# One stage for the combining of experts, the layer norm and most of h of an attention, in a two-layer graph and expert network

## The chip, the cores and the metric

The kernel runs on one core of one Trainium2 chip. The core has five engines with a program each: TensorE (PE; its weight loads have a row of their own, PEld), VectorE (DVE), ScalarE (ACT), GpSimd (POOL) and SyncE (SP), and sixteen DMA engines. Each engine runs its program in order; semaphores hold it where it needs another's result. The metric is the device time of one execution, in microseconds (us), lower is better.

## What is computed

1024 nodes with 512 features pass two layers; each is a graph step and an expert step on the layer norm of what came before. The change touches the end of the first expert step and the start of the second graph step:

```python
x = x + _L0_gnn_ref(_layernorm(x), ...)
x = x + _L0_ffn_ref(_layernorm(x)[None], ...)[0]     # 64 experts, two for each token
x = x + _L1_gnn_ref(_layernorm(x), ...)              # two attention layers of 8 heads
x = x + _L1_ffn_ref(_layernorm(x)[None], ...)[0]     # 8 experts, one for each token

# _L0_ffn_ref, after the experts:
out = jnp.einsum('bse,bsed->bsd', sparse_w, expert_out) + x
mu = out.mean(-1, keepdims=True)
var = ((out - mu) ** 2).mean(-1, keepdims=True)
return (out - mu) * jax.lax.rsqrt(var + EPS) * gamma + beta

# gat_conv in _L1_gnn_ref:
h = (x @ W).reshape(N, heads, out_ch)
a_src = jnp.einsum('nhc,hc->nh', h, att_src)
a_dst = jnp.einsum('nhc,hc->nh', h, att_dst)
e = jax.nn.leaky_relu(a_src[src] + a_dst[dst], NEG_SLOPE)
```

Everything is float32. The edges lie in a dense 1024 x 1024 matrix of counts, so the attention is dense too.

## The kernel before, in words

The nodes lie in eight tiles of 128 rows (`NT`), one row to a partition. The program is a row of stages (`nc.Block()`), each with a part for every engine, and a barrier between two stages. Order inside a stage is as written, engine by engine. The stages around the change:

- `layernorm("ln1")`, then `routing("rt0")`: TensorE makes the logits of the eight tiles, VectorE picks two experts for each token, TensorE counts ranks within the experts (L649, L651) from the picks (semaphore `s_pick`), VectorE turns them into row numbers, and GpSimd scatters the sixteen half sets of rows (L630). SP loads the weights of the first eight experts meanwhile (`first_experts`), and behind them a block of rows (L621).
- `experts("x0")` and a stage for overflowing experts (L1062 on).
- The combining stage (L1153 on). GpSimd gathers each tile's two expert rows into `yb`, four tiles ahead; TensorE makes the bias product of each tile (L1217); VectorE adds these to `xln` with their weights and takes the statistics; when all eight tiles are done, one square root, one scale, and then the tiles are scaled by gamma and added to `x`, to which GpSimd has added beta (L1187). Beside that TensorE, ScalarE and SP make the attention vectors `v1` and `v2` of both attentions (W times att): sixteen chunks of 512 columns (`chunks`) are loaded (`wc`), transposed (L1196), copied (`wct`, L1245) and multiplied (L1211). Four chunks follow each bias product from the fourth on.
- `layernorm("ln2")`: again statistics over all tiles, one square root, and eight tiles to be normed, transposed and copied to `xT`.
- `attend("a1")`: the score rows (L1640) from `v` and `xT`, their copy `aTs`, and their transposes (`ab`); then h = x W in sixteen units of 512 columns (L1673), six of them ahead of the first pair (`H0`), ten behind given pairs (`H_AFTER`). A pair is a head with a source tile, 64 in all. For each, GpSimd (L1461), ScalarE (L1474), VectorE (L1574), ScalarE (L1481) and TensorE (L1688) work one after the other, several pairs at a time; VectorE also makes the row maxima of a later head (L1568), TensorE broadcasts a later head's score row when the maxima of the head before are done (L1656), and at each head's start VectorE waits for the last product of the head before (L1583).

A matrix product in float32 leaves two records in the trace; a transpose leaves one.

## Time and profile before

| | us |
|---|---|
| median of three runs | 1403.1 |
| lowest, highest | 1400.1, 1413.2 |
| the profiled run, its own time | 1406.6 |
| its span in the trace | 1404.9 |
| TensorE busy, weight loads busy | 1075.2, 740.1 |
| VectorE, ScalarE, GpSimd busy | 761.8, 514.6, 594.8 |
| routing of the first experts, to the next stage's start | 286.4 to 347.1 |
| combining stage | 615.6 to 694.7 |
| layer norm | 695.2 to 710.2 |
| first attention | 710.5 to 963.4 |

All durations are read from one profiled execution, and times of day in the text are microseconds from its span's start. Busy time says how long an engine had an instruction running, not that it set the end: that is read from the waits.

### The profile page before, as it was taken

Reading aid. Unit: us, or ns where it says so; the run is one execution under the profiler, and the core shown is the slowest. Engines: PE = TensorE matmul, PEld = TensorE weight load, DVE = VectorE, ACT = ScalarE, POOL = GpSimd, SP = SyncE. Lnnn points to the kernel's source line nnn. Section 1 sums busy time; section 2 is a strip of 40 time slices with the busy share of each in tenths; the row PEclk is TensorE's granted clock in tenths of the full one; section 3 lists DMA queues with packets and bytes.
Section 4 is the critical chain, followed back from the end, with each engine's and each line's share of the span. In section 5 each row is a group of like instructions: output and inputs, shape, how many; then the busy total and the mean of one; then the engine's idle time right before and its main releaser. Section 6 shows DMA issues by size and latency. Waiting matters only on the chain. (4 is left out here: it accounts for less than half of the span.)

```text
span 1404.9 us, 17550 instructions
## 1 busy us (share of the span) xinstructions
PE 1075.2 (77%) x5484; PEld 740.1 (53%) x5488; DVE 761.8 (54%) x1609; ACT 514.6 (37%) x710; POOL 594.8 (42%) x471
## 2 busy tenths in 40 slices
PE   3999379650999999968398888878887887533696
PEld 2444367550777777747246777763644342132463
DVE  6888465636333333333638777751777675653134
ACT  2333433220111111101236676772466667630010
POOL 1000645105555555443026876781576777402002
PEclk9999699855999999975589999999999999855796
DMA  3000000073699999643030111101011111003974
GB/s 101 0 1 0 1 0 0 1 255 122 202 298 300 303 304 302 200 148 113 0 92 16 46 46 31 46 16 65 28 45 31 45 43 40 0 9 108 336 253 158
DMA packets 112476, 144.28 MB, mean 103 GB/s; under 512 B 30184, under 2 KB 72776, under 8 KB 112408
## 3 DMA queue, kind: packets, MB, share of 16 engines
q1 hardware_dynamic: 96168, 118.47, 26.1%
q0 software_dynamic: 14080, 21.03, 4.5%
q10 hardware_dynamic: 2160, 3.93, 0.7%
q8 instruction: 35, 0.57, 0.2%
q14 instruction: 33, 0.27, 0.1%
HBM read 138.71 MB, written 29.81 MB: 120 GB/s over the span
## 5 line engine op out<-in xcount | busy, mean ns | idle before, releaser
L1461 POOL TENSOR_TENSOR am<-CT,qb 128x1024 f32<-128x1024 f32 x128 | 299.3, 2363 | 61.7 <-ACT PT L1481 37.3
L1574 DVE TENSOR_TENSOR am<-PS,am 128x1024 f32<-128x1024 f32 x128 | 156.6, 1223 | 74.8 <-ACT PS L1474 67.1
L1474 ACT ACTIVATE PS<-adb,ab 128x1024 f32<-128x1024 f32 x128 | 142.9, 1117 | 90.5 <-DVE am L1574 90.4
L1042 DVE COPY yo<-PS 128x512 f32<-128x512 f32 x79 | 54.7, 692 | 208.9 <-PE PS L980 200.6
L1568 DVE CUSTOM_DVE_ANT_0 masked<-PS,mask 128x1024 f32<-128x1024 f32 x128 | 156.1, 1220 | 19.0 <-issue 17.3
L972 PE MATMUL PS<-xgT,w1r 128*128 128x128 f32 x1264 | 155.7, 277 | 0.0
L1007 ACT ACTIVATE hT<-PS,b1T 128x128 f32<-128x128 f32 x158 | 49.5, 364 | 288.4 <-PE PS L972 250.7
L1688 PE MATMUL PS<-h,PT 128*128 128x129 f32 x1024 | 128.3, 282 | 33.0 <-ACT PT L1481 26.4
L972 PEld LDWEIGHTS PS<-xgT,w1r 128*128 128x128 f32 x1264 | 149.2, 194 | 1.2 <-issue 1.2
L980 PE MATMUL PS<-w2r,hT 128*128 128x512 f32 x316 | 148.6, 593 | 0.1
L1481 ACT ACTIVATE PT<-am,as 128x1024 f32<-128x1024 f32 x128 | 145.2, 1134 | 0.3 <-DVE am L1574 0.3
L1688 PEld LDWEIGHTS PS<-h,PT 128*128 128x128 f32 x1024 | 122.7, 196 | 41.7 <-issue 40.5
L1701 PE MATMUL PS<-PT,h 128*65 128x512 f32 x256 | 124.9, 620 | 23.5 <-ACT PT L1481 14.3
L914 POOL DMA_INDIRECT ys_scratch<-yo,r_rowsi x64 | 65.6, 1025 | 109.0 <-DVE yo L1042 98.8
L351 DVE TENSOR_SCALAR oh_src<-iota,eT 128x1024 f16 x164 | 78.8, 480 | 17.7 <-PE PS L479 11.4
L1033 DVE COPY xgT<-PS 128x512 f32<-128x512 f32 x79 | 53.9, 683 | 54.6 <-PE PS L963 52.1
L1701 PEld LDWEIGHTS PS<-PT,h 128*65 128x65 f32 x256 | 32.9, 140 | 95.7 <-issue 79.4
L963 PEld LDWEIGHTS PS<-ident,xg 128*128 128x128 f32 x316 | 39.6, 145 | 67.6 <-issue 32.8
L980 PEld LDWEIGHTS PS<-w2r,hT 128*128 128x128 f32 x316 | 54.1, 191 | 39.2 <-issue 38.7
L479 PE MATMUL PS<-oh_src,oh_dst 128*128 x328 | 73.5, 379 | 0.9 <-DVE oh_dst L353 0.3
L909 POOL DMA_INDIRECT xg<-xs_scratch,r_rowsi x64 | 65.0, 1015 | 21.2 <-issue 20.3
L172 PE MATMUL PS<-ident,xln 128*128 128x128 f32 x96 | 20.5, 389 | 66.3 <-DVE xln L153 65.9
(308 smaller groups left out, 1601.2 us busy)
## 6 DMA issues: line engine op xcount, KB each, us to landing
w1r<-in_L_ffn_W SPq DMA_DIRECT2D x79, 512.0 KB, 6.2
w2r<-in_L_ffn_W SPq DMA_DIRECT2D x79, 512.0 KB, 7.6
adb<-a_scratch SPq DMA_DIRECT2D x16, 512.0 KB, 4.1
qb<-q_scratch SPq DMA_DIRECT2D x14, 512.0 KB, 3.7
wc<-in_L_gnn_W SPq DMA_DIRECT2D x16, 256.0 KB
xg<-xs_scratch SPq DMA_DIRECT2D x15, 256.0 KB
ys_scratch<-yo ACTq DMA_DIRECT2D x15, 256.0 KB
x_res<-in_x SPq DMA_DIRECT2D x1, 2048.0 KB, 10.5
```

The costliest lines, as they stand in the source:

```text
L351: dve.tensor_scalar(oh_src[:, bass.ds(slot, 1), c, :], iota[:], eT[:, 0, c, bass.ds(q, 1)], None, ALU.is_equal)
L479: mm = pe.matmul(PS[:, 2 * (t % 2) + h, :], oh_dst[:, bass.ds(slot, 1), c, :], oh_src[:, bass.ds(slot, 1), c, h * 512:(h + 1) * 512], star ...
L914: pool.indirect_dma_start(ys[0:rows, :], bass.IndirectOffsetOnAxis(picked[:, e:e + 1], 0), yo[:, e % 4, :], None, bounds_check=rows - 1, o ...
L972: mm = pe.matmul(PS[:, 2 + j % 2, c * P:(c + 1) * P], w1r[:, j, k, c * P:(c + 1) * P], xgT[:, j % 2, k, :], start=(k == 0), stop=(k == KD ...
L980: mm = pe.matmul(PS[:, 4 + j % 2, :], hT[:, j % 2, c, :], w2r[:, j, c, :], start=(c == 0), stop=(c == HC - 1))
L1461: pool.tensor_tensor(am[:, k % RING, :], CT[:, s, :], qb[:, hd % 2, :], ALU.add).then_inc(s_sum, 1)
L1474: act.activation(RELU, adb[:, hd % 2, :], ACT.Relu, bias=ab[:, s, hd:hd + 1]).then_inc(s_relu, 1)
L1481: act.activation(PT[:, k % PR, :], am[:, k % RING, :], ACT.Exp, bias=as02[:, s, hd:hd + 1], scale=1 - NEG_SLOPE).then_inc(s_exp, 1)
L1568: dve.tensor_tensor_reduce(masked[:], ASB, mask[:, t, :], 1.0, -3.0e38, ALU.subtract, ALU.max, mrow[:, hd % 2, t:t + 1]).then_inc(s_max, 1)
L1574: dve.tensor_tensor(am[:, k % RING, :], RELU, am[:, k % RING, :], ALU.add).then_inc(s_all, 1)
L1688: mm = pe.matmul(PS[:, d // PER, (d % PER) * (CH + 1):(d % PER + 1) * (CH + 1)], PT[:, (NT * hd + s) % PR, d * P:(d + 1) * P], h[:, s, hd, :],
L1701: mm = pe.matmul(PS[0:CH + 1, half, :], h[:, s, hd, :], PT[:, (NT * hd + s) % PR, half * 512:(half + 1) * 512], start=(s == 0), stop=(s == ...
```

## The change

The attention vectors are made in the routing, by a new class `Vectors` with the old statements. TensorE runs five of the sixteen chunks between the logits and the ranks (`V_AHEAD`), and eleven behind the ranks. All sixteen chunks have their own buffer, loaded in four pieces ahead of the experts' weights; it lies where the experts' first matrices come, so those are loaded piece by piece, each when two more chunks are transposed.

The combining stage does, tile by tile, what three stages did: sum, layer norm with gamma and beta, the next layer norm, transposes to `xT`, the scores `ab` (now tokens on partitions), the first half of h, and a quarter of h (two of the other four heads). The eighth tile's h and the last two heads stay in the attention: two units ahead of the first pair, four behind pairs (0,1), (0,4), (1,4), (2,4). `layernorm("ln2")` is gone. In the attention eight transposes of `ab` take the place of the score products. Each square root is made for one tile.

```diff
@@ routing @@
+                    if vectors is not None:
+                        vectors.turn_att(pe)
+                        vectors.products(pe, 0, V_AHEAD)
                     pe.wait_ge(s_pick, 1)
...
+                    if vectors is not None:
+                        vectors.products(pe, V_AHEAD, len(vectors.chunks))
                     pe.wait_ge(s_sw, 1)
...
+                    if vectors is not None:
+                        vectors.move(act)
                     act.wait_ge(s_tw, 1)
@@ Vectors @@
+            def products(self, pe, first, last):
+                if first == 0:
+                    self.turned(pe, 0)
+                    pe.wait_ge(self.s_attm, 1)
+                for i in range(first, last):
+                    if i + 1 < len(self.chunks):
+                        self.turned(pe, i + 1)
+                    self.summed(pe, i)
@@ first_experts @@
             for e in range(WR):
-                load_weights(sp, ins["L0_ffn_W1"], ins["L0_ffn_W2"], slice(e, e + 1), e, s_w0)
+                sp.dma_start(w2r[:, e, :, :], ins["L0_ffn_W2"][e:e + 1].rearrange("o (k p) h -> p (o k) h", p=P)
+                             ).then_inc(s_w0[e], 16)
+            for e in range(WR):
+                sp.wait_ge(vectors.s_wt, 2 * e + 2)
+                sp.dma_start(w1r[:, e, :, :], ins["L0_ffn_W1"][e:e + 1].rearrange("o (k p) h -> p (o k) h", p=P)
+                             ).then_inc(s_w0[e], 16)
@@ combining stage, gpsimd @@
+                for t in range(4):
+                    gather(t)
                 pool.wait_ge(s_gb, 32)
                 for t in range(NT):
                     pool.tensor_tensor(x[:, t, :], x[:, t, :], beta[:], ALU.add).then_inc(s_beta, 1)
+                    if t + 4 < NT:
+                        gather(t + 4)
@@ combining stage, tensor @@
+                def bias(t):
+                    if t >= 2:
+                        pe.wait_ge(s_o, t - 1)
+                    pe.matmul(PS[:, t % 2, :], r0["swT"][:, t * P:(t + 1) * P], r0["b2s"][:], start=True,
+                              stop=True).then_inc(s_bias, 1)
+
+                bias(0)
+                bias(1)
                 for t in range(NT):
+                    if t + 2 < NT:
+                        bias(t + 2)
+                    pe.wait_ge(s_xln, t + 1)
...
+                    for k in range(KD):
+                        mm = pe.transpose(PS[:, 2 + t % 2, k * P:(k + 1) * P], xln[:, t, k * P:(k + 1) * P], ident[:])
+                    mm.then_inc(s_xt, 1)
+                    pe.wait_ge(s_xtm, t + 1)
...
+                        mm = pe.matmul(PS[:, 7, t * 2 * HEADS:(t + 1) * 2 * HEADS], xT[:, k, own], v1[:, k, :],
+                                       start=(k == 0), stop=(k == KD - 1))
+                    mm.then_inc(s_ab, 1)
+                    if t == NT - 1:
+                        continue
...
+                        mm = pe.matmul(PS[:, 4 + t % 2, :], xT[:, k, own], W1t[0][:, k, :],
+                                       start=(k == 0), stop=(k == KD - 1))
+                    mm.then_inc(s_h, 1)
...
+                        mm = pe.matmul(PS[:, 6, q], xT[:, k, own], W1t[1][:, k, :],
+                                       start=(k == 0), stop=(k == KD - 1))
+                    mm.then_inc(s_hq, 1)
@@ combining stage, scalar @@
+                root(0)
+                root(1)
                 for t in range(NT):
+                    act.wait_ge(s_stat2, t + 1)
+                    act.activation(sq2[:, t:t + 1], ve2[:, t:t + 1], ACT.Sqrt).then_inc(s_sqrt2, 1)
+                    if t + 2 < NT:
+                        root(t + 2)
+                    act.wait_ge(s_rs2, t + 1)
+                    act.activation(xln[:, t, :], x[:, t, :], ACT.Identity, bias=nmr2[:, t:t + 1],
+                                   scale=rs2[:, t:t + 1]).then_inc(s_xln, 1)
+                    if t:
+                        h_moved(t - 1)
+                    act.wait_ge(s_xt, t + 1)
+                    act.copy(by_tile(xT, t), PS[:, 2 + t % 2, :].rearrange("p (k n) -> p k n", k=KD)).then_inc(s_xtm, 1)
@@ combining stage, vector @@
+                def summed(t):
+                    o = o0[:, t % 4, :]
+                    dve.wait_ge(s_bias, t + 1)
+                    dve.tensor_tensor(o, PS[:, t % 2, :], xln[:, t, :], ALU.add).then_inc(s_o, 1)
+                    dve.wait_ge(s_o, t + 1)
+                    dve.wait_ge(s_yb[t % 4], 32 * (t // 4 + 1))
...
+                summed(0)
                 for t in range(NT):
+                    if t + 1 < NT:
+                        summed(t + 1)
+                    if t:
+                        scaled(t - 1)
+                    added(t)
+                scaled(NT - 1)
@@ attend @@
+                H0 = 2
+                H_AT = (0, 1), (0, 4), (1, 4), (2, 4)
```

In the vector part, `summed(t)` has three full-width operations and three for statistics; `added(t)` makes the first norm with gamma and adds it to `x` (two full-width operations, four small ones, statistics); `scaled(t)` is five small operations that make the second norm's scale and shift.

Where instructions move, as the two programs list them. TensorE in the routing, before, from the logits (`r_wg`) to the first ranks (`r_Mb`):

```order
L641 MATMUL PS<-r_wg,xT 128x64 x32
L651 MATMUL PS<-r_Mb,before 128x64
L649 MATMUL PS<-r_Mb,onesb 128x64
L651 MATMUL PS<-r_Mb,before 128x64
L649 MATMUL PS<-r_Mb,onesb 128x64 x2
```

The same place after the change, with the chunks' transposes (`wc`) and products (`wct`) in between:

```order
L647 MATMUL PS<-r_wg,xT 128x64 x32
L894 MATMUL PS<-ident,att_3512 128x16
L895 MATMUL PS<-ident,att_3513 128x8
L903 MATMUL PS<-ident,wc 128x128 x8
L918 MATMUL PS<-att1T,wct 128x2 x4
L903 MATMUL PS<-ident,wc 128x128 x4
L918 MATMUL PS<-att1T,wct 128x2 x4
L903 MATMUL PS<-ident,wc 128x128 x4
L918 MATMUL PS<-att1T,wct 128x2 x4
L903 MATMUL PS<-ident,wc 128x128 x4
L918 MATMUL PS<-att1T,wct 128x2 x4
L903 MATMUL PS<-ident,wc 128x128 x4
```

A fifth product follows, and then the ranks: six transposed and five multiplied chunks now stand ahead of them.

TensorE at the start of the combining stage, before: four bias products (`r_b2s`), then the chunks:

```order
L1217 MATMUL PS<-r_b2s,r_swT 128x512 x4
L1221 MATMUL PS<-ident,att_5850 128x16
L1222 MATMUL PS<-ident,att_5851 128x8
L1196 MATMUL PS<-ident,wc 128x128 x8
L1211 MATMUL PS<-att1T,wct 128x2 x4
```

And after the change, tiles 0 and 1 (`v_3508` is `v1`; `W1t_6106` and `W1t_6107` are the half and the quarter of W):

```order
L1309 MATMUL PS<-r_b2s,r_swT 128x512 x3
L1321 MATMUL PS<-ident,xln 128x128 x4
L1326 MATMUL PS<-v_3508,xT 128x16 x4
L1337 MATMUL PS<-W1t_6106,xT 128x512 x4
L1342 MATMUL PS<-W1t_6107,xT 128x256 x4
L1309 MATMUL PS<-r_b2s,r_swT 128x512
L1321 MATMUL PS<-ident,xln 128x128 x4
L1326 MATMUL PS<-v_3508,xT 128x16 x4
L1337 MATMUL PS<-W1t_6106,xT 128x512 x4
L1342 MATMUL PS<-W1t_6107,xT 128x256 x4
```

The bias product of tile 3 stands behind the quarter of tile 0; each later one, up to tile 7's, behind the quarter of the tile three before it.

## Rows read from the trace of the kernel before

**Rows 1.** Table by stage: us, busy of each engine, granted clock, DMA share, GB/s.

```profile
306.00:312.00 6.00, 0.00 (x0) 0.00 (x0) 5.45 (x31) 0.00 (x0) 0.00 (x0) 0.50 1.08 366
615.60:710.40 94.80, 62.16 (x242) 49.29 (x242) 48.12 (x93) 22.41 (x42) 25.45 (x25) 0.51 0.30 95
```

**Rows 2.** Timeline, start of the combining stage: start, duration, engine, line, operation.

```profile
615.63 7.16 PE L1217 MATMUL PS<-r_b2s,r_swT 64*128 64x512 f32 x8 [8.56 <-PEq L1064]
...
622.64 0.69 DVE L1269 TENSOR_TENSOR o<-PS,xln 128x512 f32<-128x512 f32 x1 [14.84 <-DMA yb<-ys_scratch,r_posi]
```

**Rows 3.** Timeline, TensorE's h records of 512 columns in the attention's prologue.

```profile
728.83 7.89 PE L1673 MATMUL PS<-W1t,xT 128*128 128x512 f32 x18
```

**Rows 4.** Timeline, VectorE over one tile of the combining.

```profile
667.84 0.69 DVE L1269 TENSOR_TENSOR o<-PS,xln 128x512 f32<-128x512 f32 x1 [8.70 <-PE PS L1217]
668.57 0.75 DVE L1270 SCALAR_TENSOR_TENSOR o<-yb,r_top,o 128x512 f32<-128x512 f32 x1
...
670.87 0.18 DVE L1276 BATCH_NORM_AGGREGATE mv<-st 128x2 f32<-128x6 f32 x1
```

**Rows 5.** Timeline, the small operations of the norm and ScalarE's pass.

```profile
682.70 0.20 DVE L1280 RECIPROCAL tq<-sq 128x8 f32<-128x8 f32 x1 [0.27 <-ACT sq L1250]
...
683.98 5.75 ACT L1253 ACTIVATE o<-o,shift,rs 128x512 f32<-128x512 f32 x8 [1.31 <-DVE shift L1286]
```

**Rows 6.** Timeline, transposes of the layer norm and the first copy.

```profile
702.86 5.29 PE L172 MATMUL PS<-ident,xln 128*128 128x128 f32 x24 [23.89 <-DVE xln L153]
704.01 0.59 ACT L162 COPY xT<-PS 128x512 f32<-128x512 f32 x1 [2.87 <-PE PS L172]
```

**Rows 7.** Timeline of the routing: logits, last exponential, first rank, first scatter, next stage.

```profile
290.67 13.91 PE L641 MATMUL PS<-r_wg,xT 128*128 128x64 f32 x64 [5.14 <-DMA r_b2s<-in_L_ffn_b]
...
305.32 0.35 ACT L666 ACTIVATE r_lg<-r_lg,r_nm 128x64 f32<-128x64 f32 x1 [1.27 <-DVE r_nm L689]
...
312.65 0.24 PE L651 MATMUL PS<-r_Mb,before 128*128 128x64 bf16 x1 [8.06 <-DVE r_Mb L710]
...
322.91 1.31 POOL L630 DMA_INDIRECT xs_scratch<-xln,r_posi  x1 [35.48 <-DVE r_posi L744]
...
347.07 1.81 POOL L902 MEMSET xg<- 128x2048 f32 x1 [3.56 <-POOLq L614]
```

**Rows 8.** Granted clock (the third column from the end) in half microseconds.

```profile
287.50:288.00 0.50, 0.00 (x0) 0.00 (x0) 0.00 (x0) 0.20 (x1) 0.00 (x0) 0.76 1.04 234
707.50:708.00 0.50, 0.50 (x5) 0.41 (x4) 0.00 (x0) 0.28 (x1) 0.00 (x0) 0.90 0.00 0
721.00:721.50 0.50, 0.50 (x2) 0.31 (x2) 0.36 (x2) 0.00 (x0) 0.50 (x1) 0.76 0.17 25
724.50:725.00 0.50, 0.50 (x3) 0.26 (x2) 0.46 (x4) 0.00 (x0) 0.00 (x0) 0.83 0.82 336
```

**Rows 9.** Timeline of the pairs: a late row broadcast, and VectorE's waits at head starts.

```profile
830.35 0.17 DVE L1583 TENSOR_SCALAR dn<-PS 128x9 f32<-128x9 f32 x1 [5.53 <-PE PS L1688]
...
848.34 1.03 PE L1656 MATMUL PS<-a,sel 80*128 80x512 bf16 x2 [2.86 <-DVE mrow L1568]
...
860.71 0.17 DVE L1583 TENSOR_SCALAR dn<-PS 128x9 f32<-128x9 f32 x1 [8.46 <-PE PS L1688]
...
934.78 0.17 DVE L1583 TENSOR_SCALAR dn<-PS 128x9 f32<-128x9 f32 x1 [1.95 <-PE PS L1688]
```

**Rows 10.** Timeline of the attention's start: score products, and the first pair's addition.

```profile
710.50 7.03 PE L1640 MATMUL PS<-xT,v 128*16 128x512 f32 x16 [0.93 <-PEq L126]
...
744.90 1.22 DVE L1574 TENSOR_TENSOR am<-PS,am 128x1024 f32<-128x1024 f32 x1
```

**Rows 11.** Timeline, ScalarE's copy of a chunk, one of sixteen.

```profile
661.89 0.59 ACT L1245 COPY wct<-PS 128x512 f32<-128x512 f32 x1 [1.87 <-PE PS L1196]
```

**Rows 12.** Timeline, GpSimd's additions of beta and a VectorE operation beside them.

```profile
637.59 9.84 POOL L1187 TENSOR_TENSOR x_res<-x_res,beta 128x512 f32<-128x512 f32 x8
...
644.75 3.23 DVE L1270 SCALAR_TENSOR_TENSOR o<-yb,r_top,o 128x512 f32<-128x512 f32 x1
```

More of the change, by code:

```diff
@@ L613, in routing @@
             LOGP = P.bit_length() - 1
+            V_AHEAD = 5
             with nc.Block() as block:
@@ L1155, in build @@
-        s_yb, s_gb = [sem(f"c0_yb{j}") for j in range(4)], sem("c0_gb")
-        s_bias, s_sum, s_stat, s_sqrt, s_chain = (sem("c0_" + k) for k in ("bias", "sum", "stat", "sqrt", "chain"))
-        s_scale, s_norm, s_beta, s_scaled = (sem("c0_" + k) for k in ("scale", "norm", "beta", "scaled"))
+        yb = place("yb", [P, 4, TOPK, D], F32, 145 * KIB)
+        o0 = place("o0", [P, 4, D], F32, 102 * KIB)
+        gamma = place("gamma", [P, D], F32, 199 * KIB + 512)
+        beta = place("beta", [P, D], F32, 201 * KIB + 512)
@@ new lines, in build @@
+        tq2 = place("tq2", [P, NT], F32, 97 * KIB + 384)
+        rs2 = place("rs2", [P, NT], F32, 97 * KIB + 416)
+        nmr2 = place("nmr2", [P, NT], F32, 97 * KIB + 448)
+        st2 = place("st2", [P, NT, 6], F32, 97 * KIB + 480)
+        assert 97 * KIB + 480 + 4 * NT * 6 <= 98 * KIB
+        phase()
+        s_yb, s_gb, s_w1t = [sem(f"c0_yb{j}") for j in range(4)], sem("c0_gb"), sem("c0_w")
+        s_bias, s_o, s_sum, s_beta, s_chain = (sem("c0_" + k) for k in ("bias", "o", "sum", "beta", "chain"))
@@ L1158, in build @@
+        s_stat, s_sqrt, s_stat2, s_sqrt2, s_rs2 = (sem("c0_" + k) for k in ("stat", "sqrt", "stat2", "sqrt2", "rs2"))
+        s_free, s_xln, s_xt, s_xtm = (sem("c0_" + k) for k in ("free", "xln", "turned", "moved"))
+        s_ab, s_h, s_hq, s_hm, s_hqm = (sem("c0_" + k) for k in ("ab", "h", "hq", "hm", "hqm"))
         with nc.Block() as block:
@@ L1230, in _ @@
             @block.scalar
             def _(act):
-                act.wait_ge(s_attp, 1)
-                act.wait_ge(s_zero, 1)
-                act.copy(att1T[:], PS[:, 4, 0:2 * HEADS])
-                for a in range(2):
-                    for half in range(2):
-                        own = slice(half * CH2, (half + 1) * CH2)
-                        last = act.copy(att2T[own, :, 2 * a + half], PS[own, 4, 2 * HEADS + a * HEADS // 2:
-                                                                         2 * HEADS + (a + 1) * HEADS // 2])
@@ L1240, in _ @@
-                last.then_inc(s_attm, 1)
-                for i in range(len(chunks)):
-                    act.wait_ge(s_wt, i + 1)
-                    if i >= 2:
-                        act.wait_ge(s_v, i - 1)
-                    act.copy(wct[:, i % 2, :], PS[:, 5 + i % 2, :]).then_inc(s_wtm, 1)
-                act.wait_ge(s_v, len(chunks))
-                act.copy(v1[:].rearrange("p k n -> p (k n)"), PS[:, 7, 0:KD * 2 * HEADS])
-                act.copy(v2[:].rearrange("p k n -> p (k n)"), PS[:, 7, KD * 2 * HEADS:(KD + KF) * 2 * HEADS])
@@ L1397, in _ @@
                 def _(sp):
-                    for half in range(2):
+                    for half in range(2 if final else 0):
                         sp.dma_start(W[half][:], W_d.rearrange(
@@ L1526, in _ @@
                     relu(0)
-                    for i in range(H0 - 2, H0):
+                    for i in range(max(2, H0 - 2), H0):
                         h_moved(i, i % 2)
@@ L1665, in h_tile @@
                     def h_tile(i, bank):
-                        FQ = FH // 2
-                        quarter, t = (i - NT) // (NT // 2), (i - NT) % (NT // 2) * 2
-                        parts = ([(i, 0, slice(0, FH), slice(0, FH))] if i < NT else
-                                 [(t + n, 1, slice(quarter * FQ, (quarter + 1) * FQ), slice(n * FQ, (n + 1) * FQ))
-                                  for n in range(2)])
-                        for tile, half, columns_in, columns_out in parts:
+                        for tile, half, columns_in, columns_out in UNITS[i]:
                             for k in range(KI):
```

359 lines of the change are left out of this document (217 added, 142 removed).

## The prediction

> **What bounds the kernel now.** I read the busy shares and the clock line of the page first: no engine bounds the whole span, and TensorE's clock is at half in two places, the routing of the first experts and the stretch between the last expert and the attention. Those are the places that the diff rewrites. Then the table by stage: from 615.6 to 710.4 us the kernel combines the experts and makes the next layer norm; TensorE is busy 62 of 94.8 us at a granted clock of 0.51 (of 2.4 GHz), VectorE 48, ScalarE 22. In the routing, from 306 to 312, the clock is at 0.50 too [rows 1]. Last the timeline of each of these stretches and the first pairs of the attention, to see which wait ends last.
>
> **How one tile of the new stage runs.** This step decides. In the new stage TensorE's program is, for tile t: bias(t+2), transposes(t), scores(t), h(t), quarter(t), and it runs in that order. VectorE's is summed(t+1), scaled(t-1), added(t). ScalarE's xln(t) needs scaled(t), and that stands behind summed(t+2), which reads the bias product of tile t+2. This product stands in TensorE's queue behind quarter(t-1). So from tile 1 to tile 5 there is one closed chain: quarter(t-1), bias(t+2), summed(t+2), scaled(t), xln(t), transposes(t), the copy to xT, scores(t), h(t), quarter(t). Nothing in it overlaps. Its pieces:
> - bias: eight records (four products) take 7.16 us at half clock, 0.89 each [rows 2]; a full h record of the same 512 columns takes 0.44 (7.89 over 18) [rows 3]. Two records at full clock: 0.9 with the gap.
> - summed: 667.84 to 670.87 and 0.18 more is 3.2, with the small addition after it 3.4 [rows 4].
> - scaled: five small operations. Six of that kind take 1.28 (682.70 to 683.98), so 1.05. The pass over a tile on ScalarE is 5.75 / 8 = 0.72 [rows 5].
> - transposes: 1.15 at half clock from their start to the copy's; the copy 0.59 and some 0.1 to the next engine [rows 6]. At full clock ScalarE's two copies of the tile before (0.59 and an estimated 0.35 for the quarter), which stand ahead of the copy to xT, take 1.0 and set the same step.
> - scores: eight records, limited by the weight load, 13.91 / 64 = 0.217 each at half clock [rows 7]: 1.7, an estimated 0.86 at full clock.
> - h: eight records of 0.43, 3.4; quarter: half the columns, 1.7 [rows 3].
>
> At full clock throughout: 0.9 + 3.4 + 1.05 + 0.75 + 1.0 + 0.7 + 0.86 + 3.4 + 1.7 = 13.8, with the last hand-overs 13.9. But in each round TensorE has nothing to do while VectorE and ScalarE are at work, 3.4 + 1.05 + 0.75, over 5 us. Before the logits it was idle for 5.1 us, and the clock fell 2 to 2.5 us into that (at about 287.8) [rows 7, 8]; inside the attention 2.86 us of idleness are followed by the longest wait for TensorE of all heads [rows 9]. So transposes and scores are at half clock each time (+1.0). The clock then came back 3.5 us after it had fallen at 721.1, with dense h work in between, and 4.8 us after the transposes of the layer norm began (702.86 to about 707.6) [rows 6, 8]. I take 4.6 us of h at half clock, which costs half of it, 2.3. **One round: 17.2 us.** With 3.5 it is 16.7, with twice that, 7, it is 18.4.
>
> The Trainium skill (TensorE: Matmul & The Clock Gate, section HAM oscillation — how this bites in real kernels) tells of a kernel in which a wait in every tile brings the clock down every time, and so speaks against this stage. By that rule, the trace agrees (0.50 after the 5.1 us of idleness): it gives the 17.2 and not the 13.9.
>
> **The stage as a whole.** The first gathered rows are there at 622.64 [rows 2]; the bias addition no longer waits for them. summed(0) ends at 625.3; summed(1) waits for its rows and ends at 629.3; added(0), 0.79 + 0.88 + 0.79 + 1.15 = 3.6, ends at 632.9; summed(2), scaled(0), xln(0) bring 638.1. Five rounds: 638.1 + 86.0 = 724.1. Tile 5 from there: 1.15 + 0.7 + 1.7 + 5.1 + 2.3 = 11.0, so 735.1. Tile 6 needs no bias product and finds the clock up: 1.0 + 0.7 + 0.86 + 5.1 = 7.7, so 742.8. Tile 7 has only scores here: 3.0 with VectorE's copy, and 0.4 to the next stage: **746.2 against 710.5, +36** [rows 10]. What is removed is in this sum already: the old stage with its 16 chunks at 2.46 each [rows 11], the separate layer norm. The 2 MB of W1t are loaded instead of the chunks' 4 MB and are needed only after 638; the gathers share the DMA engines with them, 0 to +1.5.
>
> **Routing.** The 16 chunks move here. Logits end at 290.67 + 13.91 = 304.6, the last exponential at 305.32 + 0.5, then five small moves (an estimated 0.8) and the first chunk's copy, 0.6: summed product 0 can start at 307.6. A chunk took 0.59 + 1.87 = 2.46 on the same engines at half clock [rows 11]; the clock is at half here, and the work is the same. Five chunks ahead of the ranks end at 307.6 + 4 × 2.46 + 1.7 = 319.1. But the ranks could start at 312.65 [rows 7]: they wait **+6.5**. VectorE waits for them, then GpSimd with its 16 scatters (from 322.91) and the next stage (from 347.07) [rows 7]. The other eleven chunks: 321.7 + 27.1 = 348.8, with eight transposes and two copies 352.3, still ahead of the scatters' 353.6; SP's last first-matrix load goes out at about 345 and the row block behind it lands by 351. So these cost nothing, by a margin of one to three us: 5 to 9 for the stage. No row shows weight loads beside scatters: half a MB in two chunks' time is 107 GB/s, the scatters' 4.2 MB in 24 us are 174, together less than the 366 that the loads had alone [rows 1]; I take 0.
>
> **Attention.** Its prologue loses the 7.03 us of score products [rows 10] (in their place eight small transposes, about 1.2), 18 of 24 h products in time, and ScalarE's two late h moves. New: transposes and copy 2.5, first row broadcast 2.0, eight maxima at 1.27, second broadcast 2.0 to 3.9, five maxima 6.3: pair 0 is added 23.1 to 26 us after the start. It was 744.90 - 710.5 = 34.4 [rows 10]. **-10** (8 to 12). In the loop, what a late h unit costs is read in VectorE's wait for the last product of a head: 8.46 us at head 4's start, 5.53 at head 3's (and two others'), 1.95 at head 7's, behind a head without units [rows 9]. With units only at (0,4), (1,4), (2,4), heads 2 and 3 gain 0.5 each. Head 4 loses 3.6 of its wait, but not the 2.9 of the clock's fall, since TensorE idles before the same row broadcast, now with still less to do [rows 9]; head 5 then gets that fall too and gains 0.6. **-5** (4 to 11).
>
> Sum: +6.5 + 36 - 10 - 5 = **+27.5**. The profiled run took 1406.6 us with a span of 1404.9; the median is 1403.1. So 1403.1 + 27.5 = **1430.6**.
>
> **A cost that I leave out.** GpSimd's eight additions of beta took 9.84 us, and a VectorE operation that reads two tiles lasted 3.23 us beside them instead of 0.75 [rows 12]. The additions are now spread over the stage; the first four fall in rounds where VectorE is in summed or added, the last four run back to back while VectorE waits anyway. 0 to +5, I take 0. The Trainium skill (SBUF — State Buffer, section SBUF: two separate sides) calls this an exclusive lock for the whole instruction; by that rule, the trace agrees, eight locks of 1.23 would be 9.8 if all fell in the chain.
>
> **Rivals.**
> - *The clock stays up.* The chain holds, but with 13.9 a round: the stage ends at 638.1 + 69.5 + 7.7 + 7.7 + 3.4 = 726.4, +16, and with -15 and +6.5 it is 1410.6. For it: h and quarter are dense. Against it: 5 us of idleness in each round. 0.12.
> - *The clock never comes back* in the stage: 20.8 a round, the end at 774 (+63), 1458. Against it: 10 us of dense work in each round at half clock. 0.06.
> - *VectorE is held by GpSimd's additions* and the DMA engines by W1t: +5 to +9 on the forecast, 1438. 0.08.
> - *Faster: the tiles overlap as they are written to.* Then VectorE sets the pace with 3.4 + 3.6 + 1.05 = 8.05 a tile, the end is 638.1 + 56.4 + 3.4 = 697.9, 12.6 before the old one: 1403.1 + 6.5 - 12.6 - 15 = 1382. The point from which it decides is a round of 12.4 us, where the stage's loss is just what routing and attention leave. It needs the bias product of tile t+2 to be off TensorE's queue before h(t-1); the order listed says that it is not. 0.06.
> - *The forecast*, 0.68.
>
> **How the numbers follow.** A change of 1% (14 us) is about what a measurement can tell here; three runs spread over 13. Forecast with its terms: 1419 to 1446 (round 16.7 to 18.4, attention 12 to 22, routing 5 to 9). To leave no more than 0.2 outside, the range takes in the edge of the rival with the clock up: 1410 to 1447. Faster by over 1%: 0.06. Within 1%: the clock-up rival and a little of the forecast's edge, 0.14. Slower: 0.80.
>
> **What would show it.** In the new profile: xln tiles 17 us apart on ScalarE, VectorE waiting some 9 us of each round for the bias product, the clock near half at each transpose; the attention starts some 130 us after the stage and not 95; the first scatter at about 329; the first pair 23 to 26 us into the attention. The prediction is wrong if tiles follow each other in 8 to 12 us, or if the ranks do not wait.

## The result, and the profile after it

The changed kernel takes **1457.4 us** (median of 4 runs, 1455.6 to 1460.3). The kernel before took 1405.6 us beside it (1400.1 to 1413.2). The ratio is **1.0367, with a 95% interval of 1.0311 to 1.0422**: slower, as forecast, but by more. In the profiled executions the span goes from 1404.9 to 1453.8 us, +48.9, where the forecast has +27.5.

The table by stage of the changed kernel, cut where its stages begin: the part up to the combining stage, that stage, the first attention, the rest. Columns as in [rows 1].

```profile
0.00:622.40 622.40, 530.63 (x2793) 383.99 (x2793) 311.28 (x745) 153.96 (x305) 221.82 (x205) 0.90 0.43 142
622.40:766.93 144.53, 82.19 (x224) 46.68 (x225) 67.84 (x161) 21.25 (x47) 25.41 (x25) 0.67 0.15 47
766.93:1009.55 242.62, 181.63 (x1212) 159.97 (x1212) 168.39 (x297) 158.53 (x157) 164.44 (x112) 0.89 0.12 34
1009.55:1453.80 444.25, 314.01 (x1307) 174.25 (x1307) 234.34 (x473) 184.43 (x220) 181.58 (x130) 0.84 0.28 92
```

Before, the same cuts lie at 615.6, 710.5 [rows 10] and 963.4 us. So the routing cost +6.8, the combining stage +49.6 (144.5 for 94.9), the attention gave 10.3 (242.6 for 252.9), and what is behind it took 2.8 more. This last number is within the spread: over the kernels below, in which that part is the same code, it takes 440 to 453 us.

**Routing.** Timeline, TensorE's first rank product is at 319.52 us (312.65 in [rows 7]); the first scatter and the next stage's start:

```profile
329.77 1.31 POOL L636 DMA_INDIRECT xs_scratch<-xln,r_posi  x1 [41.24 <-DVE r_posi L757]
...
354.91 1.80 POOL L1018 MEMSET xg<- 128x2048 f32 x1 [4.59 <-POOLq L61]
```

**The new stage.** Timeline, ScalarE's xln of tiles 0 to 5:

```profile
651.45 0.81 ACT L1369 ACTIVATE xln<-x_res,nmr,rs 128x512 f32<-128x512 f32 x1 [2.46 <-DVE nmr L1429]
674.64 0.81 ACT L1369 ACTIVATE xln<-x_res,nmr,rs 128x512 f32<-128x512 f32 x1 [6.10 <-DVE nmr L1429]
692.84 0.81 ACT L1369 ACTIVATE xln<-x_res,nmr,rs 128x512 f32<-128x512 f32 x1 [0.76 <-DVE nmr L1429]
710.47 0.81 ACT L1369 ACTIVATE xln<-x_res,nmr,rs 128x512 f32<-128x512 f32 x1 [0.76 <-DVE nmr L1429]
727.82 0.81 ACT L1369 ACTIVATE xln<-x_res,nmr,rs 128x512 f32<-128x512 f32 x1 [0.76 <-DVE nmr L1429]
745.04 0.81 ACT L1369 ACTIVATE xln<-x_res,nmr,rs 128x512 f32<-128x512 f32 x1 [0.76 <-DVE nmr L1429]
```

The distances are 23.2, 18.2, 17.6, 17.4 and 17.2 us, where the forecast has 17.2 five times; and the first begins 29.1 us after the stage's start and ends at 29.9, where the forecast has its end at 22.5. The chain itself is seen at tile 2 (timeline, TensorE and what VectorE waits for):

```profile
687.28 1.12 PE L1309 MATMUL PS<-r_b2s,r_swT 64*128 64x512 f32 x2
688.44 0.69 DVE L1398 TENSOR_TENSOR o<-PS,xln 128x512 f32<-128x512 f32 x1 [10.36 <-PE PS L1309]
...
693.70 1.11 PE L1321 MATMUL PS<-ident,xln 128*128 128x128 f32 x4 [5.30 <-ACT xln L1369]
...
697.22 6.04 PE L1337 MATMUL PS<-W1t,xT 128*128 128x512 f32 x8
703.10 1.89 PE L1342 MATMUL PS<-W1t,xT 128*128 128x256 f32 x8
```

VectorE waits 10.4 us for a bias product that takes one, and TensorE then waits 5.3 us for VectorE and ScalarE. What made the first round long stands here (timeline, the small operation that makes nmr, and GpSimd beside it, for tiles 0, 1 and 2):

```profile
649.54 1.87 DVE L1429 SCALAR_TENSOR_TENSOR nmr<-mv,rs 128x1 f32<-128x1 f32 x1
650.12 1.27 POOL L1300 TENSOR_TENSOR x_res<-x_res,beta 128x512 f32<-128x512 f32 x1
...
669.10 5.50 DVE L1429 SCALAR_TENSOR_TENSOR nmr<-mv,rs 128x1 f32<-128x1 f32 x1
669.67 4.91 POOL L1300 TENSOR_TENSOR x_res<-x_res,beta 128x512 f32<-128x512 f32 x4
...
692.64 0.16 DVE L1429 SCALAR_TENSOR_TENSOR nmr<-mv,rs 128x1 f32<-128x1 f32 x1
```

One operation on 128x1 takes 0.16 us alone and 5.50 us when four additions of GpSimd run at that time; it ends when they end (669.10 + 5.50 and 669.67 + 4.91). It stands on the chain, ahead of xln(1).

**The attention.** VectorE's waits at the starts of heads 1, 2 and 3 (as in [rows 9]), and inside head 1 the h unit, the row broadcast behind it in TensorE's queue, and VectorE's next step:

```profile
824.38 0.17 DVE L1741 TENSOR_SCALAR dn<-PS 128x9 f32<-128x9 f32 x1 [1.03 <-PE PS L1853]
...
843.87 6.10 PE L1838 MATMUL PS<-W1t,xT 128*128 128x256 f32 x16 [4.65 <-ACT x2T L1652]
849.81 0.60 PE L1826 MATMUL PS<-a,sel 80*128 80x512 bf16 x2
850.45 1.22 DVE L1726 CUSTOM_DVE_ANT_0 masked<-PS,mask 128x1024 f32<-128x1024 f32 x1 [7.04 <-issue]
...
855.80 0.17 DVE L1741 TENSOR_SCALAR dn<-PS 128x9 f32<-128x9 f32 x1 [2.99 <-PE PS L1853]
...
886.72 0.17 DVE L1741 TENSOR_SCALAR dn<-PS 128x9 f32<-128x9 f32 x1 [2.99 <-PE PS L1853]
```

The waits at the head starts are as short as hoped, but heads 1 and 2 take 31.4 and 30.9 us (27.2 and 27.4 before): the wait has moved to the middle of the head, 7.0 us for the broadcast.

### The profile page after: what moved, and what is told of

It reads as the page before. It is cut to its first block and busy times, and to the rows that moved or that the text cites. A ratio compares the mean times of both kernels' runs of the same rounds, so it can differ in the third digit from the quotient of the medians.

```text
span 1453.8 us, 17691 instructions
## 1 busy us (share of the span) xinstructions
PE 1108.5 (76%) x5536; PEld 764.9 (53%) x5536; DVE 781.8 (54%) x1676; ACT 518.2 (36%) x728; POOL 593.2 (41%) x471
## 5 line engine op out<-in xcount | busy, mean ns | idle before, releaser
L1853 PE MATMUL PS<-h,PT 128*128 128x129 f32 x1024 | 134.1, 292 | 37.0 <-ACT PT L1641 32.1
L1853 PEld LDWEIGHTS PS<-h,PT 128*128 128x128 f32 x1024 | 128.0, 205 | 44.3 <-issue 25.7
L1079 PE MATMUL PS<-ident,xg 128*128 128x128 f32 x316 | 49.6, 282 | 26.1 <-DMA xg<-xs_scratch 23.0
## 6 DMA issues: line engine op xcount, KB each, us to landing
x_res<-in_x SPq DMA_DIRECT2D x1, 2048.0 KB, 10.3
```

Of the source, the lines that this page charges most:

```text
L1079: mm = pe.transpose(PS[:, j % 2, k * P:(k + 1) * P], xg[:, j % 4, k * P:(k + 1) * P], ident[:])
L1853: mm = pe.matmul(PS[:, d // PER, (d % PER) * (CH + 1):(d % PER + 1) * (CH + 1)], PT[:, (NT * hd + s) % PR, d * P:(d + 1) * P], h[:, s, hd, :],
```

## The experiments

Each was timed beside the kernel before, on the same chip, and what I compare is the ratio of the two. The changed kernel has 1.0367. Code cuts are shortened where they have `...`.

**e1: the bias product between scores and h.** The serial chain is the reason of the slowdown, or TensorE's own work at half clock is.

```
+                bias(2)
                 for t in range(NT):
-                    if t + 2 < NT:
-                        bias(t + 2)
                     ...
                     mm.then_inc(s_ab, 1)
+                    if t + 3 < NT:
+                        bias(t + 3)
```

> Only the place of the bias product in TensorE's program is changed: bias(t+3) stands between scores(t) and h(t), where bias(t+2) stood behind the quarter of tile t-1. Theory A (the serial chain of the prediction: the tiles wait for each other through this product): the chain is cut, VectorE sets the pace with about 8.1 us a tile (3.4 + 3.6 + 1.05), the starts of xln lie 8 to 9.5 us apart and not 17.2, the stage gets 40 to 50 us shorter and the kernel takes 1408 to 1420 us. Theory B (TensorE at half clock is the bound by its own work: 1.15 + 0.65 + 1.7 + 0.9 + 6.8 + 3.4 = 14.6 us a tile): the starts lie 13 to 15 us apart, the kernel takes 1438 to 1446. If the order of this product means nothing, it stays at 1457.

Measured: 1419.1 us, ratio 1.0064 (1.0025 to 1.0102). From tile 1 on the xln lie 11.0, 10.6, 10.3 and 10.3 us apart and the stage takes 107.8 us. The move of one product of 1 us took 3% off the kernel: the chain is shown. The rounds are longer than theory A had it.

**e7: the bias product of tile t+3 ahead of the transposes of tile t.**

```
+                bias(2)
                 for t in range(NT):
-                    if t + 2 < NT:
-                        bias(t + 2)
+                    if t + 3 < NT:
+                        bias(t + 3)
```

> As e1, but bias(t+3) stands ahead of transposes(t) and not between scores(t) and h(t). In e1 the tiles still lay 10.3 us apart, VectorE waited 2.7 us in each round for this product, and 5.4 us of h held some half clock. Theory A (that wait is the rest of the chain): VectorE does not wait for the product any more, TensorE's own 8.1 us (0.5 + 0.6 + 0.65 + 1.0 + 3.45 + 1.9) or VectorE's 8.1 set the pace, the rounds are 8.3 to 9.3 us, the kernel takes 1410 to 1415. Theory B (TensorE's own work with the clock falling in each round is the bound at 10.3): no difference from e1, 1419.

Measured: 1415.4 us, 1.0041 (1.0016 to 1.0066), the stage 101.1 us and so 6.7 shorter than in e1. The times alone don't tell e7 from e1, since their intervals overlap; the profiles do. The gain is all in the start: the first two xln lie 13.1 us apart and not 16.3. From tile 1 on the h products start every 10.3 us as in e1 (669.8, 680.2, 690.5, 700.8), and ScalarE's xln only runs ahead. That is theory B: TensorE's own work. In these rounds it is busy without a gap but one of 0.68 us between transposes and scores (timeline), and the clock (windows of half a microsecond, third column from the end; 1.00 is 2.4 GHz, 0.50 is 1.2) falls in h:

```profile
689.59 1.07 PE L1327 MATMUL PS<-v,xT 128*128 128x16 f32 x8 [0.68 <-ACT xT L1375]
690.51 5.38 PE L1338 MATMUL PS<-W1t,xT 128*128 128x512 f32 x8
```

```profile
689.00:689.50 0.50, 0.00 (x0) 0.00 (x0) 0.47 (x2) 0.50 (x2) 0.00 (x0) 1.00 0.00 0
690.50:691.00 0.50, 0.50 (x3) 0.28 (x3) 0.47 (x2) 0.00 (x0) 0.00 (x0) 0.84 0.00 0
691.00:691.50 0.50, 0.50 (x2) 0.31 (x1) 0.47 (x2) 0.00 (x0) 0.00 (x0) 0.50 0.00 0
694.00:694.50 0.50, 0.50 (x2) 0.15 (x2) 0.43 (x3) 0.00 (x0) 0.00 (x0) 0.75 0.00 0
```

Tiles 5 and 6 have the same gap, and there the clock stays up (tile 5, timeline; then a window inside its h):

```profile
709.06 1.06 PE L1327 MATMUL PS<-v,xT 128*128 128x16 f32 x8 [0.68 <-ACT xT L1375]
709.97 3.68 PE L1338 MATMUL PS<-W1t,xT 128*128 128x512 f32 x8
```

```profile
711.50:712.00 0.50, 0.50 (x3) 0.22 (x2) 0.43 (x3) 0.00 (x0) 0.00 (x0) 1.00 0.00 0
```

So the gap alone does not bring the clock down.

**e5: TensorE kept busy in its wait.** What the half clock costs in a round.

```
+                    for _ in range(32 if 1 <= t else 0):
+                        pe.matmul(PS[:, 7, 256:384], ident[:], ident[:], start=True, stop=True)
                     pe.wait_ge(s_xln, t + 1)
```

> Before the transposes of tiles 1 to 7 TensorE multiplies the identity by itself 32 times into columns that nobody reads (added work, some 4.8 us at full clock, in the 5.3 us in which it waits for xln). Nothing else is changed from the changed kernel. Theory A (the 17.2 us of a round are 13.9 and 3.3 of half clock, because TensorE idles while VectorE and ScalarE work): the clock stays at full from tile 2 on, the transposes last 0.6 and not 1.1 us, h 3.5 and not 6.0, the rounds are 13.9 to 14.5 us, five rounds give 14 to 16 us, the kernel takes 1440 to 1444. Rival (the clock is low here for a reason other than the idle stretch, or the added work only delays): rounds of 17.2 us or more, 1457 to 1475.

Measured: 1464.5 us, 1.0405 (1.0359 to 1.0450), no faster and not the 1440 to 1444 of theory A. But the mechanism is there (windows of one round each, from xln to xln; first e5, then the changed kernel):

```profile
691.73:707.55 15.82, 15.14 (x97) 11.75 (x96) 7.24 (x21) 2.44 (x6) 0.00 (x0) 1.00 0.00 1
```

```profile
692.84:710.47 17.63, 11.66 (x30) 6.61 (x30) 7.24 (x21) 2.55 (x6) 0.00 (x0) 0.69 0.00 0
```

The clock is full. I had the added work at 4.8 us; it took 7.4, and ended 1.93 us after xln was ready (692.54 to 694.47). Less this, a round at full clock works out at 13.9 us, just the sum of the prediction. For the tiles 6 and 7, which don't wait, the added work only delays; the stage takes 150.9 us.

**e2: all additions of beta at once, early.**

```
                 for t in range(NT):
                     pool.tensor_tensor(x[:, t, :], x[:, t, :], beta[:], ALU.add).then_inc(s_beta, 1)
-                    if t + 4 < NT:
-                        gather(t + 4)
+                for t in range(4, NT):
+                    gather(t)
```

> GpSimd makes all eight additions of beta right behind the first four gathers, about 627 to 637 us, and then issues the other four gathers; nothing else is changed. Theory A (VectorE's small operation of 5.50 us at 669.10 and that of 1.87 us at 649.54 were held by GpSimd's additions beside them): both last 0.16 us, the first round is some 17.9 us and not 23.2, the kernel is 5 to 8 us faster than the changed one, about 1450; the additions now lie beside summed(0) and may hold it by 1 to 3. Rival (the 5.50 us had another cause, such as VectorE's wait for its own chain): the operation is as long as before, no gain, 1457.

Measured: 1456.9 us, 1.0336 (1.0297 to 1.0375): not told apart from the changed kernel. Both theories missed the size of what came instead (timeline):

```profile
635.05 9.79 POOL L1300 TENSOR_TENSOR x_res<-x_res,beta 128x512 f32<-128x512 f32 x8
635.47 9.92 DVE L1401 SCALAR_TENSOR_TENSOR o<-yb,r_top,o 128x512 f32<-128x512 f32 x1 [8.13 <-DMA yb<-ys_scratch,r_posi]
```

The operation on nmr takes 0.16 us at tiles 0 and 1 and the first round is 17.5 us long, as theory A says; but the first operation on gathered rows came 0.4 us after the run of additions had begun, and waited for all eight. So VectorE does not get its turn between additions that follow each other: the price is the rest of the run that is met.

**e8: nmr with one tensor in.**

```
-                    dve.scalar_tensor_tensor(one(nmr2, t), mv2[:, t, 0:1], -1.0, one(rs2, t), ALU.mult, ALU.mult
+                    dve.tensor_scalar(one(nmr2, t), mv2[:, t, 0:1], one(rs2, t), -1.0, ALU.mult, ALU.mult
```

> The small operation that makes nmr (mean times -1/deviation, 128x1), the one that lasted 5.50 us and 1.87 us, is written as an operation with one tensor in and two scalars, and not two tensors in; nothing else is changed. Theory A (only VectorE operations that read two tensors from SBUF are held while GpSimd adds; operations with one were 0.15 to 0.69 us all along beside the additions): it takes 0.16 us, xln(0) and xln(1) come 1.7 and 5.3 us sooner, the hold moves to the product with gamma behind it, where VectorE has 10 us to spare: 1449 to 1452. Rival (any operation of VectorE that meets the run of four additions is held): 1457.

Measured: 1451.1 us, 1.0317 (1.0274 to 1.0359), an interval that overlaps the changed kernel's; the stage is 134.8 us long, 9.8 less (timeline at the run of four):

```profile
668.76 0.21 DVE L1429 TENSOR_SCALAR nmr<-mv,rs 128x1 f32<-128x1 f32 x1
668.89 5.93 DVE L1413 SCALAR_TENSOR_TENSOR o<-o,mv,gamma 128x512 f32<-128x512 f32 x1
669.34 4.93 POOL L1300 TENSOR_TENSOR x_res<-x_res,beta 128x512 f32<-128x512 f32 x4
```

The new form, at the same distance from GpSimd's work, is not held; the operation behind it, with two tensors, is. There it costs nothing, since VectorE then waits for the bias product anyway (4.0 us are left of that wait).

**e3: W1t behind the first gathers.**

```
+                for j in range(4):
+                    sp.wait_ge(s_yb[j], 32)
                 sp.dma_start(W1t[0][:], W_d[:, :, 0:FH1]).then_inc(s_w1t, 16)
```

> The three loads of W1t (2 MB) are issued only when all rows of the first four gathers have landed; nothing else is changed. Theory A (the first gathered rows came 4 us late, 10.3 us after the stage's start where it was 6.3, because W1t shares the DMA engines with them): the first rows are there at 6 to 7 us, xln(0) comes 3 to 4 us sooner, W1t lands 10 to 14 us behind the gathers and still before h(0), the kernel takes 1453 to 1455. Rival 1 (the gathers are late for a reason of their own): no difference. Rival 2 (W1t now ends last before h(0)): up to 5 us slower than the changed kernel.

Measured: 1455.0 us, 1.0327 (1.0291 to 1.0364). The interval overlaps the changed kernel's; the profile shows the stage at 138.8 us, 5.8 less, and the first operation on gathered rows 7.6 us after the stage's start instead of 11.0:

```profile
631.79 0.75 DVE L1403 SCALAR_TENSOR_TENSOR o<-yb,r_top,o 128x512 f32<-128x512 f32 x1 [4.79 <-DMA yb<-ys_scratch,r_posi]
```

Since this also moves the meeting with the additions, the 5.8 us are not the DMA engines' alone.

**e4: the h units away from the broadcast.**

```
-                H_AT = (0, 1), (0, 4), (1, 4), (2, 4)
+                H_AT = (0, 1), (0, 4), (1, 1), (2, 1)
```

> The h units of the first attention stand behind pairs (0,1), (0,4), (1,1), (2,1) and not (0,1), (0,4), (1,4), (2,4); nothing else is changed. Theory A (heads 1 and 2 take 31.4 and 30.9 us, where they took 27.2 and 27.4, because a unit at pair 4 stands ahead of the next row broadcast in TensorE's queue, which VectorE waits for, 7.0 us): both heads take 26 to 28 us, the kernel is 7 to 9 us faster than the changed one, 1448 to 1450. Rival (the clock, which falls in those heads anyway, makes the difference, wherever the unit stands): less than 3 us.

Measured: 1448.8 us, 1.0285 (1.0242 to 1.0329). The attention takes 231.4 us instead of 242.6, heads 1 and 2 take 23.8 and 24.0 us, 2 to 4 less than expected and 3.5 less than in the kernel before; heads 3 and 4 take 25.4 and 25.6, some 1.5 more than in the changed kernel. The rival (less than 3 us) is out: the unit in its new place runs in 3.62 us (6.10 above), and the broadcast 10 us later has nothing ahead of it. Up to 2.5 of the 7 us that each head gains may be the unit's own clock; the run doesn't part that from the order.

```profile
833.00 3.62 PE L1838 MATMUL PS<-W1t,xT 128*128 128x256 f32 x16
...
843.52 0.60 PE L1826 MATMUL PS<-a,sel 80*128 80x512 bf16 x2 [1.11 <-DVE mrow L1726]
...
849.52 0.17 DVE L1741 TENSOR_SCALAR dn<-PS 128x9 f32<-128x9 f32 x1 [2.08 <-PE PS L1853]
```

**e6: two chunks ahead of the ranks and not five** (V_AHEAD = 2).

> Two of the 16 chunks stand ahead of the ranks and not five; nothing else is changed. Theory A (the ranks wait 6.8 us for the chunks ahead of them, but all 16 chunks together fill TensorE up to the end of the stage): the ranks start at 312.6 and the first scatter goes out at 323 instead of 329.8, but the chunks behind them end at about 352, so the next stage starts 0 to 2 us sooner only: 1455 to 1457. Theory B (only the ranks' delay counts, as the prediction has it): 6 to 7 us faster than the changed kernel, 1450 to 1451.

Measured: 1462.6 us, 1.0380 (1.0339 to 1.0422), no gain. The first scatter goes out at 323.3 us, 6.5 sooner, and the next stage starts at 358.1, 3.1 later than with five (timeline; the last scatter was issued at 342.9, 14.2 us before):

```profile
345.47 1.87 PE L918 MATMUL PS<-att2T,wct 128*128 128x4 f32 x8 [6.43 <-ACT wct L944]
...
358.06 1.80 POOL L1018 MEMSET xg<- 128x2048 f32 x1 [14.18 <-POOLq L61]
```

Theory A, and worse: the chunks end later, and with them the last first-matrix load and the row block that wait for them (the block is issued at 351.2 us; 342.4 with five ahead). Part of this comes from a stretch in which ScalarE stood still for 8.7 us ahead of one chunk's copy, and TensorE waited 6.4 us for that copy; the profile does not show what held ScalarE. So the stage is 7.8 us longer than before with five chunks ahead and 11.0 with two, and what it would be with two and without that stretch is not shown.

**c1: e4, e7 and e8 together.**

> Three edits that were tried alone, together: bias(t+3) ahead of transposes(t) (e7), nmr made with one tensor in (e8), units of the first attention behind (0,1), (0,4), (1,1), (2,1) (e4). If the terms are separate: e7's 1415.4, less 7 to 11 for the attention (e4 took 231.4 us for it and not 242.6), less 1.7 to 4 for the held operation (with the tiles 8 to 10 us apart VectorE has little to spare, so part of the hold stays): 1400 to 1407, level with the kernel before. If the gains share one cause, they don't add, and it is 1410 or more.

Measured: 1394.8 us, **0.9905 (0.9873 to 0.9937)**, faster than the kernel before, and below the 1400 to 1407 expected. The stage takes 98.6 us, the attention 225.4.

**c2: c1 and e3.**

> As c1, and the loads of W1t wait for the first four gathers (e3). If the gain of e3 (the stage 144.5 to 138.8 us in the profiled spans, 2.5 us in the medians) stays: 1.5 to 5 us below c1. If W1t now comes last, because the first h starts sooner: level with c1 or up to 3 us slower.

Measured: 1393.1 us, 0.9892 (0.9858 to 0.9926), the stage 90.7 us; the gain over c1 is within the intervals.

**c3: five additions ahead of the third gather, the others one by one.**

> As c2, but GpSimd adds beta to five tiles between the second and the third gather, while VectorE still waits for the first rows, and to the other three one by one between the last gathers; W1t waits for the first two gathers. Theory A (a GpSimd addition costs VectorE its own length, 1.0 to 1.7 us, wherever an operation with two tensors from SBUF meets it, and nothing where VectorE waits): no operation of VectorE is held for more than 1.1 us, the stage gets 3 to 6 us shorter than in c2. Rival (the later gathers of tiles 2 and 3 cost what the additions gave back, or TensorE is the bound behind tile 1): level with c2.

Measured: 1398.4 us, 0.9920 (0.9887 to 0.9952), no better than c2, and in the profile the stage is 8.5 us longer (99.1). Its ten runs lie between 1386.8 and 1404.7, far wider apart than c2's, and the profiled one is the slowest, so the 8.5 us may not hold for the others. My reading of the wait was wrong: with W1t out of the way the first rows land in time to meet the run of additions.

```profile
628.17 6.12 POOL L1299 TENSOR_TENSOR x_res<-x_res,beta 128x512 f32<-128x512 f32 x5
630.03 4.81 DVE L1411 SCALAR_TENSOR_TENSOR o<-yb,r_top,o 128x512 f32<-128x512 f32 x1 [4.57 <-DMA yb<-ys_scratch,r_posi]
```

**c4: c3 with TensorE's gaps filled.**

```
+                    if t == 0:
+                        pe.wait_ge(s_stat2, 1)
+                        for _ in range(10):
+                            pe.matmul(PS[:, 7, 256:384], ident[:], ident[:], start=True, stop=True)
                     pe.wait_ge(s_xln, t + 1)
                     ...
+                    for _ in range(3):
+                        pe.matmul(PS[:, 7, 256:384], ident[:], ident[:], start=True, stop=True)
                     pe.wait_ge(s_xtm, t + 1)
```

> As c3, with work added on TensorE that nobody reads: ten products of the identity with itself before the first transposes, and three in the 0.68 us between the transposes and the scores of every tile. In e7 h lasted 5.38 us and not 3.5, because the clock fell in each round 1.9 us after that gap. Theory A (gap and idle start bring the clock down): h(0) lasts 3.5 to 4.5 us and not 5.3, the others 3.5 to 3.7; rounds of 8.2 to 8.8 us instead of up to 10.3; 8 to 12 us faster than c3. Rival (the short gap does not matter; what lowers the clock is that transposes and scores are thin work): h stays at 5.4, level with c3 or 1 to 2 us slower.

Measured: 1387.6 us, 0.9863 (0.9829 to 0.9897). From tile 1 on h takes 3.68 us (5.38 in tiles 1 to 3 of c3) and h products start 8.6 us apart: here theory A holds. The added products keep the clock up; that the gap is what had brought it down is not shown (tiles 5 and 6 of e7). h(0) still takes 6.41 us, so the ten products ahead of it did not do their part. The median is 11 us below c3's, but the three best runs of c3 lie in c4's range.

**e9: e3, e4 and e8 on the changed kernel, the bias product as the change has it.**

> The changed kernel with e3 (W1t behind the first gathers), e4 (units behind (1,1) and (2,1)) and e8 (nmr with one tensor in) together; the bias product stays where the change put it, so the serial chain of 17.2 us a round is untouched. Theory A (the miss of the forecast is these costs, and they are separate): 1457.4 less 2.5, 8.6 and 6.4, that is 1440, with the rounds still 17.1 to 17.4 us apart. Rival (they overlap, for instance because the wait that e3 takes away is hidden behind the additions): 1443 to 1447.

Measured: 1428.6 us, 1.0184 (1.0143 to 1.0224), a larger gain than expected. xln(0) comes 20.5 us after the start, the rounds are 17.8, 17.5, 17.3, 17.2 and 17.1 us, the stage 129.1 us, the attention 231.3 (windows):

```profile
622.22:751.34 129.12, 80.39 (x224) 45.96 (x225) 65.21 (x161) 21.25 (x47) 27.82 (x25) 0.69 0.17 53
751.34:982.62 231.28, 174.80 (x1212) 153.65 (x1212) 168.38 (x297) 158.31 (x157) 164.46 (x112) 0.91 0.13 35
```

**e10: e9 without the additions of beta** (they are left out, so its output lacks beta).

> As e9, and GpSimd's eight additions of beta are left out (the output lacks beta): the gathers are all that GpSimd does. Theory A (what is left of the additions' cost is the holds of 0.7 to 1.7 us on the two-tensor operations ahead of xln(0), three or four of them): xln(0) comes 3 to 5 us sooner than in e9, the rounds stay 17.1 to 17.4, the kernel takes 1435 to 1437, some 5 us above the forecast. Rival (the additions cost nothing any more): level with e9.

Measured: 1427.7 us, 1.0184 (1.0135 to 1.0234): the rival. xln(0) comes at 19.5 us and not 20.5, but the first round is 20.0 us and not 17.8; 1.5 of these 2.2 us are h(0), which now waits for W1t, and 0.5 is h(0) itself, 6.68 us long for 6.17. So e10 shows no gain from leaving the additions out, but it does not price them free of that wait.

**c5: c2 with TensorE's gaps filled.**

> As c2 (the additions of beta where the change put them), with the products of c4 that fill TensorE's gaps. Theory A (in c3 and c4 the run of five additions held VectorE's first operation on gathered rows for 6.4 and 4.8 us, and the later gathers of tiles 2 and 3 cost more; the filled gaps give their 11 us to either): xln(0) comes 19 to 21 us after the stage's start as in c2, the rounds are 8.6 us as in c4, the kernel takes 1380 to 1384. Rival (the gaps filled and the additions are the same time twice): level with c4, 1388.

Measured: 1385.0 us, **0.9888 (0.9846 to 0.9931)**: a little above the 1380 to 1384 expected, and not told apart from c4 (or c2) by its time. By its profile the stage is the shortest of all, 84.6 us (94.9 in the kernel before), although a run of four additions still holds VectorE for 5.9 us in round 1. TensorE has no idle time left, at full clock (windows, from xln(3) to xln(4)); its h products start 8.6 us apart, 0.8 of which are the filling:

```profile
669.75:677.54 7.79, 7.79 (x34) 4.54 (x33) 7.20 (x21) 2.55 (x6) 0.00 (x0) 1.00 0.00 1
```

## Why the prediction was wrong in size, point by point

**The serial chain: right.** 17.2 us a round was measured from tile 4 to 5, and 17.1 to 17.8 in all rounds of e9; 13.9 at full clock follows from e5; cutting the chain in e1 gave 3%. From the end of xln(5) to the next stage it took 21.1 us as against 22.1. I had the half-clock part of h at 4.6 us of time; h took 6.04 instead of 3.68, so 2.4 us lost as against 2.3.

**The step that failed is "A cost that I leave out", with its claim that the last four additions run back to back "while VectorE waits anyway".** They run when GpSimd gets past its last gather, which waits for summed(3), and so at the very moment of scaled(1), on the chain. It cost 5.3 us in round 1 (5.50 for 0.16, e8), and the single additions ahead of xln(0) held four more operations by 0.5 to 1.7 us each, 4.3 together. The Trainium skill (SBUF — State Buffer, section SBUF: two separate sides) has the lock taken by whoever starts first, for the whole instruction; a VectorE operation with two SBUF inputs is subject to it. The trace agrees on which operations are held (two tensors, e8), and differs on how long: four and eight instructions, not one (5.50 us in the changed kernel, 9.92 in e2). Nor does it bear out who wins: the record of the held operation begins 0.57 us ahead of that of the additions (669.10 and 669.67), though GpSimd's spans are rough. I had the 3.23 us of [rows 12] and the order of both engines, and took the value 0 of 0 to +5 without laying the two side by side. The rival with this mechanism and the DMA engines was priced at +5 to +9 with a chance of 0.08; it happened, and at about +14 in this stage: 144.5 us against 130.6. By the rows, the held operations are 9.6 of these 13.9 us and the late first rows 4.0. A rival of another kind comes out at the measured time by chance: with a clock that never comes back I had 1458, but by rounds of 20.8 us, and they are 17.2 to 18.2 behind the first.

**W1t beside the gathers: mis-sized.** 0 to +1.5 was the term. The first operation on gathered rows started 11.0 us after the stage and not 7.0, and in e3 7.6. The DMA engines moved 371 to 417 GB/s from 628 to 634 us (windows of 2 us), where in the kernel before they moved 292 and 325 from 618 to 622, with chunk loads of 256 KB that went out one by one. The prediction gave no sum for this term: it set the 366 of [rows 1] against loads in the routing alone.

**Attention: -10.3 for -15.** The prologue gave 6.6 (pair 0 is added 27.8 us after the start and not 23 to 26: both row products and the broadcast of q ran at half clock, 3.8, 3.8 and 3.5 us). The loop gave 3.7 and not 5. Here "heads 2 and 3 gain 0.5 each" was the wrong step: I read the cost of an h unit in the wait for a head's last product alone, and the same unit, moved to pair 4, stands ahead of the row broadcast. Heads 1 and 2 lost 4.2 and 3.5 us; heads 3 and 4 gained 6.4 and 3.5. e4 gives 11 us in this attention for two numbers changed.

**Routing: right**, 6.8 for 6.5. "These cost nothing, by a margin of one to three us" was too kind: the next stage began 7.8 us later and not 6.5, and with two chunks ahead (e6) it did not begin sooner.

**The sum.** With the three costs taken away and the chain left, e9 gives a ratio of 1.0184; the forecast of 1430.6 over 1403.1 is 1.0196. In e9's profile the stage takes 129.1 us, where the forecast has 130.6: with the chain as forecast, the three costs were the miss of the stage. That the ratios agree so closely is luck in part. e9's attention gives 21.6 us and not 15, since e4 puts the units in better places than the prediction had, and up to the attention's end that profile is 19.2 us longer than the one before, not 27.5. How much each cost gives alone is known only by overlapping intervals (1.0327, 1.0285 and 1.0317, from 1.0367).

## What to carry to other kernels

Write down, for each wait that the sum calls free, which operation of the other engine falls into it, and when its own queue lets it run: two engines that hold each other are priced by their order, and not by their busy time. In a stage that runs tile by tile, a product that any engine needs for tile t+2 is issued ahead of the long work of tile t, not behind that of tile t-1; look for it in the queue of the engine that looks idle, not of the one that waits. And of a unit of work that is moved to fill a gap, ask what stands next behind it in that queue, and who waits for that.

## What the runs showed of the hardware

- A VectorE operation that reads two tensors from SBUF is held for the whole rest of a run of GpSimd additions, whatever its own size: 5.50 us for 128x1 beside four additions (0.16 alone), 9.92 us for 128x512 beside eight (0.75 alone). The one with a tensor and scalars (`tensor_scalar`) took 0.21 us at the same place, and the operation that reads PSUM and SBUF 0.69 us beside the eight of [rows 12]. Issues of gathers on GpSimd alone held nothing (0.74 us beside one, in e10).
- In e7 every tile has a gap of 0.68 us between transposes and scores. In tiles 1 to 4 part of the dense work behind it ran at half clock (h 5.38 us); in tiles 5 and 6, and in e5 behind the added products, the clock stayed up across the same gap (h 3.68 us). Three products in the gap kept it up in tiles 1 to 4 too (c4, c5), though nobody reads them. What else brought it down in tiles 1 to 4 is open.
- With 2 MB of loads beside them (the changed kernel, e5) the first VectorE operation on gathered rows came 11.0 and 9.6 us after the stage's start; with those loads held back, 7.6 us in e3 and 5.7 and 5.8 in e9 and c5. In the kernel before, with smaller loads beside the gathers, the first rows were there at 7.0 us.
